# A cross-attention and mixture-of-experts kernel: the second layer's shared products in two halves, and batch 2 routed by itself

## The chip, the core and the metric

The kernel runs on one core of one Trainium2 chip. The metric is the time of one execution on the device, in microseconds. The core has five engines that run side by side: TensorE (PE, matrix products, with its weight loads shown as PEld), VectorE (DVE), ScalarE (ACT), GpSimd (POOL) and SyncE (SP, which here issues most DMAs). Each engine works through its own instructions in the order in which they are written; between engines there are only semaphores.

## The reference

1024 tokens (4 batches of 256) of width 256 pass through four stages, each added to the running sum: attention over a 1601-token context, a mixture of experts (16 experts, 6 per token), a 16-head attention over the same context, and a second mixture of experts with 16 experts of width 128, two per token, and a shared expert of width 256 that every token passes. The change lies in the last stage and at the end of the third:

```python
def _L1_ffn_ref(x, router_w, router_bias, Wu, Wg, Wd, Su, Sg, Sd):
    flat = x.reshape(Bx * Tx, D)
    logits = flat @ router_w.T
    scores = jax.nn.softmax(logits, axis=-1)
    _, topk_idx = jax.lax.top_k(logits + router_bias, TOPK)      # TOPK = 2
    topk_scores = jnp.take_along_axis(scores, topk_idx, axis=-1)
    topk_scores = topk_scores / topk_scores.sum(-1, keepdims=True)
    ...
    for e in range(N_EXPERTS):                                    # 16
        h = jax.nn.silu(flat @ Wu[e]) * (flat @ Wg[e])
        out = out + combine[:, e:e + 1] * (h @ Wd[e])
    for s in range(N_SHARED):                                     # 1
        out = out + jax.nn.silu(flat @ Su[s]) * (flat @ Sg[s]) @ Sd[s]
x = x + _L1_xattn_ref(_layernorm(x), ...)
x = x + _L1_ffn_ref(_layernorm(x), ...)
```

## The kernel before

**Attention of the third stage.** Its work is cut into 16 jobs (4 batches of 4 groups of 4 heads), a job into 13 tiles of 128 context tokens: 208 tiles x. For each tile TensorE forms scores (`qk`, L881), ScalarE takes the exponential (L1279), VectorE clips it (`clip`, L1659) and TensorE multiplies it with the values four tiles later (`pv`, L915). Three PSUM buffers of scores and six buffers of exponentials link them. After a job VectorE copies the product out (`evac`, tile oS, L1665), TensorE transposes it (`flip`, L923) and VectorE divides (`norm`, tile cx).

**What happens to a finished batch.** While the next batch runs, the functions `between` of each engine fit the finished batch's rest between the tiles, by a written table of tile numbers o (0 to 51 within a batch): transposes of cx (`ctx_T`), the output product (`ctx_out`, L937), bias (`delta`, L1681), its statistics, scale and sum (`delta_gamma` L1695, `delta_add` L1701), the mean of the sum (`rows_mean`, L1710), the normalized rows xe (`rows`, L1718) and their transposes (`rows_T`, L944) into xTh (ScalarE, `rows_hi`, L1259) and xTl (VectorE, `rows_lo`, L1723), the two parts of a split 32-bit number. The inverse roots are computed by GpSimd in small steps (`inverse_root`, L351 to L359); VectorE waits for them in `delta_add` and `rows`. One batch later come the router products (`logits`, L646 to L648), the choice of two experts per token (15 operations, L1744 to L1768), TensorE's counts of earlier tokens (`ranks`, L960, L963), the slot numbers (`slots_of`, `slots_to`, L1772 to L1780), and GpSimd's scatters of the rows into DRAM slots sorted by expert (`rows_out`, L621): two 128-token tiles of a batch, two experts each, are four scatters.

**The end.** Batch 3 has nothing to hide behind. Its steps follow each other in the open, and the choice of batch 2 is made together with it, over four tiles, with eight scatters. The shared expert comes in the same place. Its two weight tiles are loaded into e_w when all attention is done; GpSimd splits them into sh_hi and sh_lo (L633, L635). TensorE starts all output banks with 16 products of zeros (L1015), then runs four chunks n (weight tile n // 2, tokens 512 (n % 2) and the 511 behind them): six gate products, six up products (`shared_hidden`), and 12 down products of the chunk before (`shared_down`). ScalarE and VectorE make silu, h, hh and hl of each chunk. In between VectorE computes the table of blocks: 31 blocks of up to 128 slots of one expert, of which SyncE reads its row numbers and TensorE its expert numbers. VectorE then computes the mixing weights (softmax, L1920 to L1930) and adds the shared output to resid (L1934). Only when that is done (`add_rdy` 8) does TensorE take the first block: transposes of its rows (`slots_T`, L1064), gate and up (L1078), transpose (L1086), down (L1092). VectorE copies the block out (yb, L1949), GpSimd scatters it to the tokens (L641). After the last one SyncE loads the rows back (yg) and VectorE mixes them, two operations a tile (L1963, L1965), into resid, which is stored.

Of the kernel before, what the change touches and what calls it, by code (L numbers as in the profile page):

```python
# [15 lines left out]
F32 = mybir.dt.float32  # L16
F32R = mybir.dt.float32r
# [59 lines left out]
def build(nc, a, out, stop="D"):  # L77
# [8 lines left out]
    with ExitStack() as ctx:  # L86
# [76 lines left out]
        with ExitStack() as s:  # L163
# [8 lines left out]
            wq_raw = C("wq_raw", [P, KT, D])  # L172
            wqh, wql = C("wqh", [P, KT, D], F32R), C("wql", [P, KT, D], F32R)
            wo_raw = C("wo_raw", [P, KT, D])
# [8 lines left out]
        with ExitStack() as s:  # L183
# [6 lines left out]
            silu_d = Dt("silu_d", [P, 2, 512])  # L190
            h32_d = Dt("h32_d", [P, 2, 512])
            hh_d, hl_d = Dt("hh_d", [P, 2, 512], F32R), Dt("hl_d", [P, 2, 512], F32R)
# [6 lines left out]
            Dt("gap2", [P, 400])  # L199
            sh_hi, sh_lo = Dt("sh_hi", [P, NSH1, WC], F32R), Dt("sh_lo", [P, NSH1, WC], F32R)  # L200
            Dt("gap3", [P, 13500])
# [9 lines left out]
            m_c, m_t, m_p, m_e, m_l = (Dt(n, [P, NT, E]) for n in ("m_c", "m_t", "m_p", "m_e", "m_l"))  # L211
# [8 lines left out]
            eb_f = Dt("eb_f", [P, NBLK])  # L220
            eb_i = Dt("eb_i", [P, NBLK], I32)
            eb_r = Dt("eb_r", [P, NBLK])
            tok = Dt("tok", [P, NT])
            y_c = Dt("y_c", [P, NBLK])
            y_i = Dt("y_i", [P, NBLK], I32)
            first_row = Dt("first_row", [P, E])
            aside = Dt("aside", [P, NBLK])
            ob, rb_f = Dt("ob", [P, NBLK]), Dt("rb_f", [P, NBLK])
            rb_i = Dt("rb_i", [P, NBLK], I32)

        cTxh, cTxl = (t[:].rearrange("p k n -> p (k n)").rearrange("p (q n) -> p q n", n=512) for t in (xTh, xTl))
        dlt = xn
        cTf = wq_raw[:].rearrange("p k n -> p (k n)")
# [128 lines left out]
        def _(sp):  # L362
# [154 lines left out]
            for g in range(NG - 1):  # L517
                queries(0, g)
            for job in range(KSL, NJ):
# [11 lines left out]
            for k in range(NSH1):  # L531
                sp.dma_start(e_w[:, k, :], a["w1"][k]).then_inc(d_in[0], 16)
# [30 lines left out]
        def _(pool):  # L563
# [87 lines left out]
        def _(pe):  # L651
# [315 lines left out]
            def between(y):  # L967
# [10 lines left out]
                if 0 <= b < NB - 1:  # L978
# [24 lines left out]

            t = NT - 2
# [1023 lines left out]
```

## Time and profile before

| | us |
|---|---|
| median of 3 runs | 817.32 (817.09 to 819.99) |
| the profiled execution | 816.02 |
| its span, first to last instruction | 814.2 |
| PE busy | 707.8 (87%) |
| DVE busy | 543.3 (67%) |
| ACT busy | 396.5 (49%) |
| POOL busy | 160.1 (20%) |
| attention of the third stage, first to last exponential | 463.8 to 686.5 |
| first expert block taken up by PE | 741.05 |
| last block copied out | 795.37 |

Busy time is an average over stages with different limits. A matmul's record includes its way through the array, so records of successive products overlap; the chain of waits gives each only the time up to the next. The granted clock of TensorE is given as a share of full speed: 1.0 is 2.4 GHz, 0.50 is 1.2 GHz. Its mean over the span is 0.95.

### The profile page before, as it was taken

How to read it: one execution, taken by the hardware profiler on the slowest of the kernel's cores; microseconds unless marked ns; L12 is line 12 of the kernel's file. 1: busy time of each engine (PE TensorE's matmuls, PEld its weight loads, DVE VectorE, ACT ScalarE, POOL GpSimd, SP SyncE). 2: the span in 40 equal slices, each digit the busy share in tenths (PEclk: the TensorE clock that was granted, in tenths of full speed). 3: DMA queues.
4: the chain of work that ended last, by engine and by line, in shares of the span. 5: the costliest groups of instructions: out<-in, count | busy, mean ns of one | idle time of the engine just before them, and what ended most of it. 6: DMA issues, size and time to landing. Idle time of an engine off the chain costs nothing.

```text
span 814.2 us, 14794 instructions
## 1 busy us (share of the span) xinstructions
PE 707.8 (87%) x5481; PEld 537.1 (66%) x5481; DVE 543.3 (67%) x1124; ACT 396.5 (49%) x558; POOL 160.1 (20%) x196
## 2 busy tenths in 40 slices
PE   4799999897859999999995599998998997587990
PEld 3689888796648888888885344454554554475880
DVE  6765565656676666666676377778888886655663
ACT  2624333233312322223322499999999996114540
POOL 5452625030100000000000000004024024231561
PEclk9999999998989999999998789999999998698995
DMA  7465464735306776767779369898687700812545
GB/s 231 129 208 214 162 220 130 270 104 178 96 23 221 238 248 206 262 211 245 240 172 198 60 112 191 133 127 166 96 137 144 108 2 30 345 53 74 162 144 180
DMA packets 57532, 131.67 MB, mean 162 GB/s; under 512 B 12433, under 2 KB 32785, under 8 KB 53889
## 3 DMA queue, kind: packets, MB, share of 16 engines
q1 hardware_dynamic: 54208, 123.46, 57.1%
q0 software_dynamic: 2256, 6.18, 2.1%
q10 hardware_dynamic: 1008, 1.25, 0.5%
q8 instruction: 37, 0.61, 0.4%
q14 instruction: 23, 0.18, 0.1%
HBM read 78.92 MB, written 48.79 MB: 157 GB/s over the span
## 4 chain that ended last, share of the span: by engine, by line
PE 53%; DVE 15%; issue 10%; ACT 9%; POOL 7%; DMA 4%; SPq 1%; POOLq 0%; DVEq 0%; ACTq 0%
PE ps L646 13%; PE ps L647 13%; PE ps L648 13%; ACT p L1279 5%; PE ps L915 5%; PE ps L881 3%; POOL y_tokens L641 3%; DVE p L1659 2%; DMA raw<-in_ctxT 1%; PE ps L1078 1%; DMA raw<-in_ctxN 1%; ACT cNh L1156 1%; PE ps L937 1%; PE ps L723 1%; POOL na L354 1%
## 5 line engine op out<-in xcount | busy, mean ns | idle before, releaser
L1279 ACT ACTIVATE p<-ps,kbias 128x1024 f32<-128x1024 f32 (+1 forms) x208 | 210.5, 1184 | 6.2 <-PE ps L881 6.2
L1659 DVE TENSOR_SCALAR p<-p 128x1024 f32<-128x1024 f32 (+1 forms) x208 | 142.6, 692 | 40.0 <-ACT p L1279 38.4
L915 PE MATMUL ps<-p,vsl 128*17 128x256 f32 (+1 forms) x1664 | 116.7, 392 | 3.6 <-DVE p L1659 3.6
L881 PEld LDWEIGHTS ps<-qst,kst 48*128 48x128 f32 (+1 forms) x832 | 60.4, 187 | 67.3 <-issue 34.6
L881 PE MATMUL ps<-qst,kst 48*128 48x256 f32 (+1 forms) x832 | 93.4, 324 | 11.5 <-DMA qst<-ql 5.9
L1219 ACT ACTIVATE hh<-h 128x512 fp32r<-128x512 f32 x50 | 31.6, 632 | 137.7 <-DVE h L1591 113.9
L351 POOL TENSOR_SCALAR nv<-mv 128x2 f32<-128x2 f32 x6 | 3.4, 561 | 423.7 <-DVE mv L1691 407.7
L646 PE MATMUL ps<-xTh,w_hi 128*128 128x512 f32 x200 | 80.0, 400 | 5.2 <-DVE h L1587 4.5
L648 PE MATMUL ps<-xTh,w_lo 128*128 128x512 f32 x200 | 79.3, 397 | 0.0
L647 PE MATMUL ps<-xTl,w_hi 128*128 128x512 f32 x200 | 79.2, 396 | 0.0
L915 PEld LDWEIGHTS ps<-p,vsl 128*17 128x17 f32 (+1 forms) x1664 | 37.2, 98 | 43.0 <-issue 9.1
L1593 DVE TENSOR_TENSOR hl<-h,hh 128x512 fp32r<-128x512 f32 x50 | 34.6, 692 | 36.6 <-ACT hh L1219 36.6
L646 PE MATMUL ps<-w_hi,hh 128*128 128x256 f32 x200 | 57.5, 288 | 1.5 <-DVE hl L1593 1.5
L1587 DVE TENSOR_TENSOR h<-silu,ps 128x512 f32<-128x512 f32 x50 | 34.4, 688 | 35.4 <-PE ps L648 23.2
L647 PE MATMUL ps<-w_lo,hh 128*128 128x256 f32 x200 | 57.2, 286 | 0.0
L648 PE MATMUL ps<-w_hi,hl 128*128 128x256 f32 x200 | 57.0, 285 | 0.0
L646 PEld LDWEIGHTS ps<-xTh,w_hi 128*128 128x128 f32 x200 | 37.9, 190 | 13.5 <-DVE h L1587 5.8
L589 POOL TENSOR_TENSOR cNl<-raw,cNh 128x1024 fp32r<-128x1024 f32 (+1 forms) x16 | 31.3, 1980 | 77.8 <-ACT cNh L1156 77.8
L648 PEld LDWEIGHTS ps<-xTh,w_lo 128*128 128x128 f32 x200 | 37.8, 189 | 9.0
L647 PEld LDWEIGHTS ps<-xTl,w_hi 128*128 128x128 f32 x200 | 37.9, 189 | 6.6
L646 PEld LDWEIGHTS ps<-w_hi,hh 128*128 128x128 f32 x200 | 38.7, 193 | 4.2 <-DVE hl L1593 1.9
L1215 ACT ACTIVATE silu<-ps 128x512 f32<-128x512 f32 x50 | 29.9, 598 | 21.6 <-PE ps L648 20.9
(290 smaller groups left out, 1530.0 us busy)
## 6 DMA issues: line engine op xcount, KB each, us to landing
x_slots<-blank SPq DMA_DIRECT2D x20, 1032.0 KB, 6.0
kst<-k_hi SPq DMA_DIRECT2D x64, 200.2 KB, 7.8
w_raw<-in_w SPq DMA_DIRECT2D x25, 384.0 KB, 3.6
v_one<-vst SPq DMA_DIRECT2D x4, 1768.0 KB, 9.0
vsl<-v_one SPq DMA_DIRECT2D x4, 1768.0 KB, 16.5
kst<-k_lo SPq DMA_DIRECT2D x32, 200.2 KB, 8.2
raw<-in_ctxN SPq DMA_DIRECT2D x12, 512.0 KB, 5.6
k_hi<-kh SPq DMA_DIRECT2D x24, 256.0 KB, 2.6
```

Source lines behind the costliest of these rows:

```text
L589: pool.tensor_tensor(cNl[:, c0:c0 + w, :], src, cNh[:, c0:c0 + w, :].bitcast(F32), ALU.subtract).then_inc(ctx_split, 1)
L646: e.matmul(o, lh, rh, start=first, stop=False, skip_group_check=True)
L647: e.matmul(o, lh, rl, start=False, stop=False, skip_group_check=True)
L648: return e.matmul(o, ll, rh, start=False, stop=last, skip_group_check=True)
L881: mm = pe.matmul(ps[0:rows, 2 * (x % RING) + t, c * SEQ:(c + 1) * SEQ], kst[r, job % KSL, c, m * P:m * P + rows], qst[r, b, 2 * g + c, :], ...
L915: mm = pe.matmul(ps[32 * j:32 * j + VW, 6 + job % 2, 0:SEQ], vsl[0:rows, b % 2, at_:at_ + VW], p32[0:rows, x % PBUF, (2 * t + c) * SEQ:(2 ...
L1215: act.activation(silu[:, half, :], ps[:, 4, :], ACT.Silu).then_inc(silu_rdy, 1)
L1219: act.activation(hh[:, half, :], h32[:, half, :], ACT.Copy).then_inc(hh_rdy, 1)
L1279: act.activation(p32[0:rows, x % PBUF, :], psf[0:rows, bank * 512:bank * 512 + 1024], ACT.Exp, scale=0.25, bias=kbias[0:rows, col:col + 1] ...
L1587: dve.tensor_tensor(h32[:, half, :], silu[:, half, :], ps[:, 5, :], ALU.mult).then_inc(mul1_rdy, 1)
L1593: dve.tensor_tensor(hl[:, half, :], h32[:, half, :], hh[:, half, :].bitcast(F32), ALU.subtract).then_inc(hl_rdy, 1)
L1659: dve.tensor_scalar(t, t, CLO, CHI, ALU.max, ALU.min).then_inc(p_clip, 1)
```

## The change

1. The shared weights are loaded at the start of the third stage's attention (SyncE, behind three groups of queries and ahead of keys(3)) into the tile xn, which is free then. VectorE splits them in job 2, tiles m = 2 to 9, one part per tile; GpSimd splits none.
2. In `between`, the mean of a batch's sum moves from o = 39 to 38, `rows` from 43 and 45 to 45 and 46, `rows_T` on TensorE from 49 to 51, `rows_hi` from 49 to 50, `rows_lo` from 50 to 51.
3. Batch 2 is chosen and ranked by itself (`choose`, two tiles), ahead of batch 3's `delta`; its four scatters are issued before batch 3's.
4. Tokens 0 to 511 get their gate and up products around the last transposes, and their down products after the counts. The 16 products of zeros go: each output is a full accumulation of its own now. Their sums (`shared_add` 0 and 1) stand ahead of the blocks.
5. Tokens 512 to 1023 get theirs behind the last block. The exponential and the mixing weights move there too; the sums of these tokens stand between the mix of tile 3 and that of tile 4.

```diff
+            sp.wait_ge(sc_rdy, 1)
+            for k in range(NSH1):
+                sp.dma_start(sh_raw[:, k * WC:(k + 1) * WC], a["w1"][k]).then_inc(d_in[0], 16)
             for job in range(KSL, NJ):
...
             sp.wait_ge(cx_rdy, NJ)
-            for k in range(NSH1):
-                sp.dma_start(e_w[:, k, :], a["w1"][k]).then_inc(d_in[0], 16)
...
-            for k in range(NSH1):
-                pool.wait_ge(d_in[0], 16 * NSH1)
-                pool.tensor_copy(sh_hi[:, k, :], e_w[:, k, :]).then_inc(d_w, 1)
-                pool.wait_ge(d_w, 2 * k + 1)
-                pool.tensor_tensor(sh_lo[:, k, :], e_w[:, k, :], sh_hi[:, k, :].bitcast(F32), ALU.subtract).then_inc(d_w, 1)
+            rows_out(NB - 1, NT - 4, NT - 2)
             pool.wait_ge(ln_xn, 4 * NT)
-            rows_out(NB - 1, NT - 4, NT)
+            rows_out(NB, NT - 2, NT)
...
-                    elif o == 49:
+                    elif o == 51:
                         pe.wait_ge(cx_rdy, y // MT)
                         rows_T(t, 2, spare)
...
+            logits(NB - 2, ps[:, 5, :])
             pe.wait_ge(cx_rdy, NJ)
             for j in range(2):
                 ctx_T(t + j, 1, ps[:, j, :])
-            logits(NB - 2, ps[:, 7, :])
             for j in range(2):
                 ctx_out(t + j, j, 1, ps[:, 2 + j, 0:D])
+            ranks(NB - 1, NT - 4, NT - 2, ps[:, 1, :])
+            pe.wait_ge(d_w, 8)
+            gates(0, 0, 4)
+            ups(0, 0, 5)
+            gates(0, 1, 6)
+            pe.wait_ge(dl_ev, NT)
             for j in range(2):
-                rows_T(t + j, 1, ps[:, 4 + j, :])
-            logits(NB - 1, ps[:, 7, 2 * E:])
-            for n in range(4 * 4):
-                pe.matmul(psf[:, n * P:(n + 1) * P], zero[:], zero[:], start=True, stop=False, skip_group_check=True)
+                rows_T(t + j, 1, ps[:, 2 + j, :])
+            ups(0, 1, 0)
+            logits(NB - 1, ps[:, 7, :])
+            pe.wait_ge(pre_ev, NB - 1)
+            ranks(NB, NT - 2, NT, ps[:, 1, :])
+            pe.wait_ge(lg_ev, NB)
+            all_counts(ps[:, 7, 2 * E:3 * E])
+            pe.wait_ge(hl_rdy, SC0 + 2)
+            shared_down(0, 2)
-            shared_hidden(0)
-            ranks(NB - 1, NT - 4, NT, ps[:, 6, :])
-            all_counts()
-            for n in range(1, 2 * NSH1):
-                shared_hidden(n)
-                shared_down(n - 1)
-            shared_down(2 * NSH1 - 1)
...
-            pe.wait_ge(add_rdy, 8)
             for j in range(-2, NBLK + 1):
...
+            gates(1, 0, 0)
+            ups(1, 0, 1)
+            gates(1, 1, 2)
+            ups(1, 1, 3)
+            pe.wait_ge(hl_rdy, SC0 + 4)
+            shared_down(1, 4)
...
-                    elif o == 39:
+                    elif o == 38:
                         rows_mean(b)
-                    elif o == 43:
+                    elif o == 45:
                         rows(t)
-                    elif o == 45:
+                    elif o == 46:
                         rows(t + 1)
-                    elif o == 50:
+                    elif o == 51:
                         rows_lo(t, 2, spare)
...
+                if job == 2 and 2 <= m < 10:
+                    (shared_hi if m < 6 else shared_lo)(m)
...
+            choose(t - 2, t, ps[:, 5, :])
             for j in range(2):
                 delta(t + j, 1, ps[:, 2 + j, :])
...
+            shared_mul(0, 5)
+            choose(t, NT, ps[:, 7, :])
+            shared_mul(1, 0)
...
             for t in range(NT):
+                if t == NT // 2:
+                    shared_add(2, 4)
+                    shared_add(3, 5)
```

Here `gates(h, k, bank)` and `ups(h, k, bank)` are six products each with weight tile k for token half h, and `shared_down(h, bank)` 24 products over both weight tiles.

TensorE, from the last output product to the counts, in the kernel before (wo_raw: output weights; xe: normalized rows; gwh_d: router weights; zero: zeros; sh_hi: shared weights; sel: the choice):

```order
L937 MATMUL ps<-wo_raw,wq_raw 128x256 x4
L944 MATMUL ps<-ident,xe 128x128 x4
L646 MATMUL ps<-gwh_d,xTh 128x16
...
L1015 MATMUL ps<-zero 128x128 x16
L646 MATMUL ps<-xTh,sh_hi 128x512
...
L960 MATMUL ps<-sel,upper 128x64
```

And in the changed kernel:

```order
L939 MATMUL ps<-wo_raw,wq_raw 128x256 x4
L962 MATMUL ps<-sel,upper 128x32
...
L648 MATMUL ps<-xTh,sh_hi 128x512
L649 MATMUL ps<-xTl,sh_hi 128x512
L650 MATMUL ps<-xTh,sh_gl 128x512
...
L946 MATMUL ps<-ident,xe 128x128 x4
...
L648 MATMUL ps<-gwh_d,xTh 128x16
...
L962 MATMUL ps<-sel,upper 128x32
```

Batch 2's ranks and 18 shared products moved ahead of the last transposes; six more stand behind them, and nothing but the router products stands between those and batch 3's ranks.

VectorE, from the last division to the statistics of batch 3, in the kernel before (cx: attention output; xn: delta):

```order
L1677 TENSOR_TENSOR cx<-ps,r4 128x2x64
L1681 SCALAR_TENSOR_TENSOR xn<-ps,rs,bo 128x256
L1686 BN_STATS st6<-xn 128x6
L1681 SCALAR_TENSOR_TENSOR xn<-ps,rs,bo 128x256
```

And in the changed kernel (m_l to sel: the choice of batch 2):

```order
L1695 TENSOR_TENSOR cx<-ps,r4 128x2x64
L1778 COPY m_l<-ps 128x32
L1782 TENSOR_TENSOR m_c<-m_l,gb_d 128x32
L1786 TENSOR_REDUCE m_top<-m_c 128x2
L1787 TENSOR_TENSOR m_t<-m_c,m_top 128x32
...
L1802 TENSOR_TENSOR sel<-one1,one2 128x32
L1699 SCALAR_TENSOR_TENSOR xn<-ps,rs,bo 128x256
```

Fifteen operations of the choice have come between cx and delta.

VectorE behind the last block copies, in the changed kernel; before, the mix followed the copies (yb) at once:

```order
L1985 COPY yb<-ps 128x256 x3
L1929 TENSOR_TENSOR h32_d<-silu_d,ps 128x512 x2
L1933 TENSOR_TENSOR hl_d<-h32_d,hh_d 128x512 x2
L2000 TENSOR_REDUCE m_sum<-m_p 128x8
...
L2010 TENSOR_TENSOR m_w2<-m_w2,m_top 128x8
L2019 SCALAR_TENSOR_TENSOR resid<-yg,m_w1,resid 128x256
```

The second half's h and hl and eleven operations of the mixing weights now stand between the copies and the mix.

## Rows read from the trace of the kernel before

**Rows 1.** Timeline, ScalarE: start us, us, engine, line, operation, idle before it and releaser.
```profile
569.40 0.60 ACT L1259 ACTIVATE xTh<-ps 128x512 fp32r<-128x512 f32 x1 [0.53 <-PE ps L944]
...
625.72 0.60 ACT L1259 ACTIVATE xTh<-ps 128x512 fp32r<-128x512 f32 x1 [1.16 <-PE ps L944]
...
682.75 0.60 ACT L1259 ACTIVATE xTh<-ps 128x512 fp32r<-128x512 f32 x1 [1.79 <-PE ps L944]
684.41 2.11 ACT L1279 ACTIVATE p<-ps,kbias 128x1024 f32<-128x1024 f32 x2 [1.06 <-PE ps L881]
```

**Rows 2.** Timeline, VectorE: batch 2's first rows, and the last copy oS.
```profile
678.68 0.41 DVE L1718 TENSOR_SCALAR xe<-resid,mv,rstd 128x256 f32<-128x256 f32 x1 [2.02 <-POOL rstd L359]
...
689.05 0.42 DVE L1665 COPY oS<-ps 128x256 f32<-128x256 f32 x1 [1.60 <-PE ps L915]
```

**Rows 3.** Page, costliest groups: line, operation, xcount, busy us, mean ns, idle before.
```profile
L1593 DVE TENSOR_TENSOR hl<-h,hh 128x512 fp32r<-128x512 f32 x50 | 34.6, 692 | 36.6 <-ACT hh L1219 36.6
```

**Rows 4.** Chain that ended last, 686 to 741 us: start us, us in chain, what.
```profile
693.75 0.49 DVE xn L1681
...
702.43 1.28 ACT L1292
...
712.85 0.43 PE ps L646
...
718.24 0.17 DVE pos_i L1780
...
730.29 0.23 PE ps L646
```

**Rows 5.** Lines L1695 and L1701 (min/median/max ns), then the timeline beside them.
```profile
L1695 DVE SCALAR_TENSOR_TENSOR xn<-xn,mv,gam x8: 477/480/2024, 550.6 to 696.2; 128x256 f32<-128x256 f32 x8
...
L1701 DVE SCALAR_TENSOR_TENSOR resid<-xn,rstd,resid x8: 478/485/2016, 555.6 to 699.1; 128x256 f32<-128x256 f32 x8
...
699.00 1.86 POOL L635 TENSOR_TENSOR sh_lo<-e_w,sh_hi 128x768 fp32r<-128x768 f32 x1
...
702.65 0.74 DVE L1718 TENSOR_SCALAR xe<-resid,mv,rstd 128x256 f32<-128x256 f32 x2
```

**Rows 6.** Timeline, VectorE: first and last of the 15 operations of the choice.
```profile
708.00 0.22 DVE L1744 COPY m_l<-ps 128x64 f32<-128x64 f32 x1 [2.89 <-PE ps L648]
...
711.54 0.23 DVE L1768 TENSOR_TENSOR sel<-one 128x64 fp32r<-128x64 f32 x1
```

**Rows 7.** Timeline: first and last of eight scatters, first block loads, first block.
```profile
719.28 1.01 POOL L621 DMA_INDIRECT x_slots<-xe,pos_i  x1 [18.42 <-DVE pos_i L1780]
...
728.22 1.01 POOL L621 DMA_INDIRECT x_slots<-xe,pos_i  x1 [0.30 <-issue]
...
731.76 3.73 SPq L544 DMA_DIRECT2D xb<-x_slots  x4
...
741.05 1.12 PE L1064 MATMUL ps<-ident,xb 128*128 128x128 f32 x4 [4.75 <-DVE resid L1934]
```

**Rows 8.** Chain around the mixing weights, then VectorE's timeline of the tail.
```profile
735.50 0.30 DVE m_sum L1920
...
738.51 2.49 DVE resid L1934 x4
...
794.95 0.42 DVE L1949 COPY yb<-ps 128x256 f32<-128x256 f32 x1 [0.16 <-PE ps L1092]
...
803.27 0.48 DVE L1963 SCALAR_TENSOR_TENSOR resid<-yg,m_w,resid 128x256 f32<-128x256 f32 x1 [7.89 <-DMA yg<-y_tokens]
...
811.12 0.48 DVE L1965 SCALAR_TENSOR_TENSOR resid<-yg,m_w,resid 128x256 f32<-128x256 f32 x1
```

**Rows 9.** A stretch (PE, PEld, DVE, ACT, POOL busy; PEclk, DMA share, GB/s); DMA issues to landing.
```profile
698.00:700.00 2.00, 0.00 (x0) 0.00 (x0) 1.96 (x4) 0.00 (x0) 1.92 (x2) 0.50 1.03 415
...
e_w<-in_w SPq DMA_DIRECT2D x2, 3072.0 KB, 17.1
...
raw<-in_ctxN SPq DMA_DIRECT2D x4, 128.0 KB, 3.6
```

More of the change, by code:

```diff
@@ L1002, in _, with gates, ups, shared_down @@
             flip(NJ - 1)
+            def gates(h, k, bank):
+                s = slice(h * 512, h * 512 + 512)
+                for q in range(KT):
+                    w = slice(q * 2 * P, q * 2 * P + P)
+                    mm = mm3(pe, ps[:, bank, :], sh_hi[:, k, w], sh_gl[:, k, w], xTh[:, q, s], xTl[:, q, s], q == 0, q == 1)
+                mm.then_inc(G_rdy, 1)
+            def ups(h, k, bank):
+                s = slice(h * 512, h * 512 + 512)
+                for q in range(KT):
+                    w = slice(q * 2 * P + P, (q + 1) * 2 * P)
+                    mm = mm3(pe, ps[:, bank, :], sh_hi[:, k, w], sh_gl[:, k, w], xTh[:, q, s], xTl[:, q, s], q == 0, q == 1)
+                mm.then_inc(U_rdy, 1)
+            def shared_down(h, bank):
+                for j in range(4):
+                    o = ps[:, bank + j // 2, (j % 2) * D:(j % 2 + 1) * D]
+                    s = slice(j * P, (j + 1) * P)
+                    for k in range(NSH1):
+                        mm = mm3(pe, o, hh_d[:, 2 * h + k, s], hl_d[:, 2 * h + k, s],
+                                 sh_hi[:, k, 2 * D:3 * D], sh_dl[:, k, :], k == 0, k == NSH1 - 1)
+                mm.then_inc(down_done, 1)
+            def all_counts(o):
+                for t in range(NT):
+                    mm = pe.matmul(o, ones[:], sel[:, t, :], start=t == 0, stop=t == NT - 1, skip_group_check=True)
+                mm.then_inc(pre_rdy, 1)
             t = NT - 2
+            logits(NB - 2, ps[:, 5, :])
             pe.wait_ge(cx_rdy, NJ)
@@ L1033, in shared_down @@
-            def shared_down(n):
-                k, half = n // 2, n % 2
-                pe.wait_ge(hl_rdy, SC0 + n + 1)
-                for j in range(4):
-                    t, s = 4 * half + j, slice(j * P, (j + 1) * P)
-                    mm = mm3(pe, ps[:, t // 2, (t % 2) * D:(t % 2 + 1) * D], hh_d[:, half, s], hl_d[:, half, s],
-                             sh_hi[:, k, 2 * D:3 * D], sh_lo[:, k, 2 * D:3 * D], False, False)
-                mm.then_inc(down_done, 1)
-            def all_counts():
-                cnt = ps[:, 7, 4 * E:5 * E]
-                for t in range(NT):
-                    mm = pe.matmul(cnt, ones[:], sel[:, t, :], start=t == 0, stop=t == NT - 1, skip_group_check=True)
-                mm.then_inc(pre_rdy, 1)
@@ L1268, in between @@
                         ctx_ev(t, 2, spare)
-                    elif o == 49:
+                    elif o == 50:
                         rows_hi(t, 2, spare)
@@ L1854, in _, with choose @@
             b, t = NB - 1, NT - 2
+            def choose(t0, t1, o):
+                logits_ev(t0, t1, o)
+                biased(t0, t1)
+                max_equal(t0, t1)
+                max_first(t0, t1, one1)
+                take_first(t0, t1)
+                max_equal(t0, t1)
+                max_first(t0, t1, one2)
+                take_both(t0, t1)
+            choose(t - 2, t, ps[:, 5, :])
             for j in range(2):
```

175 lines of the change are left out of this document (93 added, 82 removed).

## The prediction, on record before the changed kernel ran

> **What bounds the kernel now.** I read the timeline of each engine around the last attention tiles first, then the chain of waits from there to the end, then the timeline of the scatters and of the last 20 us. In attention ScalarE's exponentials run nearly without a gap; the reader should look for the places where they do not. ScalarE waits for the transposes of a finished batch's normalized rows: 0.53, 1.16 and 1.79 us in front of the copies xTh, and another 1.06 us behind the last one [rows 1]. Their cause is one wait further back: VectorE stood 2.02 us for the root that GpSimd computes [rows 2]. I call A the start of VectorE's last copy oS, 689.05 [rows 2], and A' the same point of the changed kernel. From A everything is one chain of small steps: delta of the last batch starts at A+4.70 [rows 4], its normalized rows end at 703.39 = A+14.34 [rows 5], the slot numbers at 718.41 = A+29.36 [rows 4]; GpSimd issues eight scatters; SyncE fetches the first block at 731.76 = A+42.71, and TensorE takes it up only at 741.05 = A+52.00 [rows 7], because the shared sum of VectorE ends at 738.51+2.49 = 741.00 [rows 8]. The expert blocks run to 795.37, the mix to 811.60 [rows 8], and the span ends at 814.2. So TensorE's shared products are no longer hidden work: they stand in front of the slot numbers and in front of the first block.
>
> The sums below are against the profiled execution: 816.02 us, its span 814.2 and 1.8 around it. The median of the runs is 817.32, 1.3 more, and I add that at the end.
>
> **1. Attention.** For batches 0 to 2 the mean moves one tile earlier and the rows two tiles later, so the root gets three tiles (3 us) more; it was 2.02 us late. TensorE transposes two tiles later, ScalarE copies one tile later. I expect no wait for the root. In batch 2 the 1.79 + 1.06 = 2.85 us go, and some 0.5 us of the products that queued up behind the stall before the last 1.60 us wait [rows 2]: 3.3 us. In batches 0 and 1, 0.53 + 1.16 = 1.7 us stand in the rows; I count 1.2. Against it: the shared weights are split on VectorE now, four casts and four subtractions of 512 and 256 columns in eight tiles of job 2. A subtraction of 512 takes 692 ns [rows 3]; the 256-wide ones at half and casts no dearer make 0.69 x 6 = 4.2 us at most, while clip and exponential leave about 0.3 us per tile, 2.4 us in eight tiles. A backlog of 2 us is more than one tile, and I charge 0.7 us (bounds 0, where the ring of six buffers takes it up, and 3). Their loads stand on SyncE's queue before keys(3), which are wanted a dozen tiles later: nothing. Gain 3.8 us.
>
> **2. From A to the last rows.** GpSimd splits no weights here any more. Two kinds of fused operation, xn and resid, take 480 and 485 ns in the median, but their slowest took 2024 and 2016 ns, with GpSimd's sh_lo subtraction of 1.86 us beside them [rows 5]. Over the four of batch 3 that is 5.2 us instead of 1.95, so 3.26 us go. The Trainium skill (SBUF — State Buffer, "Who interferes with whom") says that a VectorE instruction with two SBUF inputs and a GpSimd one that reads SBUF shut each other out for the whole instruction; by that rule the trace agrees, and all of it goes. The other reading would be the expert weights' DMA, which fills all 16 queues in these microseconds (share 1.03, [rows 9]); under it the two xe operations still took 0.74 us together [rows 5], so I don't take it.
> The choice of batch 2 now stands between cx and delta on VectorE. Fifteen operations of the choice over four tiles took 708.00 to 711.77, 3.77 us [rows 6]; over two tiles each is some 35 ns shorter, 3.25 us. TensorE's router product for it comes first after the flip and ends near A+2.3, so the choice ends at A+5.65, and delta, ready at A+4.1, starts 0.95 later than A+4.70. ctx_T waits 0.5 us behind the router products and stays hidden. The rows end at 14.34 - 3.26 + 0.95 = A+12.0; 0.2 us for joints: gain 2.1 us.
>
> **3. From the rows to the slot numbers.** Before, 15.0 us, with TensorE's 16 zero products in them, and then the first gate and up products at the low clock (0.43 us each in the chain against 0.23 at the high one, [rows 4]) in front of the ranks. Now the gate and up products of tokens 0 to 511 run from about A+6.5: 18 x 0.23 = 4.2 us before the last transposes, ending near A+10.7, when TensorE waits for the rows anyway, and six more (1.4 us) beside ScalarE's table load and the two xTl. What stays in the chain: transposes, table load and copies to the last xTl 1.75 (as before), router products 1.35, choice 3.25, TensorE's ranks or VectorE's product h 0.95, three slot operations and their links 0.87, three more 0.65, joints 0.2: 9.0 us. Gain 6.0 us. It needs TensorE at the high clock through A+10.
>
> **4. Scatters.** Eight scatters start 1.277 us apart (719.28 to 728.22 is seven steps, [rows 7]). Four of them, batch 2's, now start near A+15.6 and are issued by A+20.7, before batch 3's slot numbers at A+21. Four fewer in the chain: 5.1 us. VectorE's block table (5.5 us, after two hl of 1.4 us) ends 1.3 us before the last scatter lands, so it is hidden, just. SyncE is let go at 42.71 - 2.1 - 6.0 - 5.1 = A'+29.5. Expert weights are issued behind cx and land 17.1 us later [rows 9], before that.
>
> **5. From SyncE's release to the first block.** Before, 9.29 us [rows 7], nearly all of it shared products. Now only the slot rows' own load counts. The trace doesn't show its landing; a load of 128 KB took 3.6 us [rows 9], and it cannot be below 0. I take 3.0: gain 6.3 us (bounds 5.7 and 9.3). The first-half sums (2 x 0.62 us) end near A'+30. All blocks together I leave at 795.37 - 741.05 = 54.3 us.
>
> **6. The tail.** Here the change pays. L is the end of the last block's copy, 795.37; the first pair of the mix started at 803.27 = L+7.9 and the last ended at L+16.2 [rows 8], waiting for transfers, with TensorE idle. Now 24 products of 0.23 us start near L-0.4 and end at L+5.3; h, hh and hl of the last chunk (about 0.7 each) end at L+7.5; 24 down products of half the columns, 2.8 us, end at L+10.3. Beside these ScalarE loads the exponential's table (1.28, as the table load of [rows 4]) and VectorE computes the mixing weights: L+8.4 + 3.0 (735.50 to 738.51, [rows 8]) = L+11.4. Then four tiles of mix 3.7, two sums 1.25, four tiles 3.7: L+20.1. Cost 3.9 us; down products and transfers are covered.
>
> **Sum.** 3.8 + 2.1 + 6.0 + 5.1 + 6.3 - 3.9 = 19.4 us; 816.02 - 19.4 = 796.6, and against the median 817.32 it is 797.9 us.
>
> **Rivals.**
> (a) Low clock. With TensorE idle between the delta products and the transposes the granted clock fell to 0.50 [rows 9], 1.2 GHz, and the chain's gate products then cost 0.43 us [rows 4]. Against it: TensorE's idle time before its shared products falls to about 1.7 us, for the choice of batch 2. If it does happen, 18 products end at A+14.2, 2.2 us after the rows, and six gate products, router products and ranks cost 2.5 more: 4.7, so 802.6. Chance 0.13.
> (b) Attention gives nothing: the backlog of the split stalls ScalarE for 3 us and the moved transposes only shift their wait. 3.8 is lost: 801.7; with a small loss beside, 803. Chance 0.10.
> (c) The early scatters don't get out of the way: their rows queue behind the expert weights in full DMA engines until about A+18, GpSimd is held, and eight scatters stand in the chain as before. +5.1: 803.0. Chance 0.07. The Trainium skill has a rule on this side (SBUF — State Buffer, the "DVE blocks DMA" warning): VectorE copies can lock GpSimd out of writing descriptors. Here the eight scatters kept their even steps beside a busy VectorE; by that rule a few tenths of a microsecond might come on each, within (c).
> (d) The slow fused operations were the DMA's: 3.3 us stay: 801.2. Chance 0.04.
> (e) Slower than before: TensorE enters the blocks after about 6 us of idling (A'+25.5 to A'+32) where it was 4.75 [rows 7], and stays at the low clock in the loop. A block is 54.3/31 = 1.75 us and TensorE-bound at the high clock; at the low one about 1.6 us are added. From 12 of 31 blocks on the 19.4 are gone; with 16, 823. Against it: the loop before started from idling as well and took hardly more than its steady pace. Chance 0.03.
>
> **How the numbers follow.** Forecast 0.63 (795 to 800.5), (a) to (e) as above. Likeliest time 797.9. The range goes down by the transfer's other bound and attention's full 1.7, to 793.5, and up to take in (a) to (c): 803.5. A measurement of this kernel tells about 0.5% (4 us) from no change; faster by more holds in all cases but (e) and unforeseen ones: 0.95; within 0.5%: 0.02; slower 0.03.
>
> **What would show it.** No ScalarE gap over 0.5 us at the xTh copies; A' at 684 to 686; no fused operation above 0.6 us behind it; TensorE's clock 1.0 during the gate products; batch 2's four scatters issued before batch 3's slot numbers; the first block 31 to 34 us behind A'; the last mix 19 to 21 us behind the last block copy. A first block later than A'+37, or TensorE at 0.5 in the loop, would make the forecast wrong.

## The result, and the profile after

The changed kernel takes 796.06 us (median of 4 runs, 794.48 to 798.38) where the one before took 817.21 beside it: a ratio of 0.974, with a 95% interval of 0.970 to 0.978. Six further runs on another chip gave 798.49 (795.26 to 799.97) and 0.9747 (0.9716 to 0.9778). The forecast was 797.9, the range 793.5 to 803.5. The profiled execution took 794.68 us; its span is 792.8, 21.4 shorter than before.

I cut both spans at the same points: the start of attention (ScalarE's first exponential), A (the last copy oS), the end of the last normalized rows xe, the last slot numbers pos_i, the first block on TensorE, L (the end of the last block's copy) and the last mix.

| stretch | before | after | gain | forecast |
|---|---|---|---|---|
| up to the start of attention | 463.76 | 465.42 | -1.66 | 0 |
| attention, to A | 225.29 | 218.32 | 6.97 | 3.8 |
| A to the last rows | 14.34 | 11.65 | 2.69 | 2.1 |
| rows to slot numbers | 15.02 | 10.03 | 4.99 | 6.0 |
| slot numbers to first block | 22.64 | 10.99 | 11.65 | 5.1 + 6.3 |
| blocks, to L | 54.32 | 53.89 | 0.43 | 0 |
| L to the last mix | 16.23 | 19.96 | -3.73 | -3.9 |

The sum is 21.3; the rest is behind the last mix. Nothing was changed ahead of the start of attention: it lies between 463.6 and 467.6 us in the fourteen profiled executions of this document, so the -1.66 is spread between executions. The page's busy times (busy us, share of the span, instructions by engine) read:
```profile
PE 708.5 (89%) x5471; PEld 537.7 (68%) x5471; DVE 544.1 (69%) x1153; ACT 394.7 (50%) x557; POOL 163.3 (21%) x192
```
TensorE is busy for 708.5 us where it was for 707.8, now 89% of the shorter span. But for the 16 products of zeros the work is the same, so what went was waiting. ScalarE's timeline of the changed kernel at the three copies xTh, which answers to [rows 1]:
```profile
571.33 0.70 ACT L1268 ACTIVATE xTh<-ps 128x512 fp32r<-128x512 f32 x1
...
625.94 0.70 ACT L1268 ACTIVATE xTh<-ps 128x512 fp32r<-128x512 f32 x1
...
680.60 0.67 ACT L1268 ACTIVATE xTh<-ps 128x512 fp32r<-128x512 f32 x1
681.09 1.18 ACT L1288 ACTIVATE p<-ps,kbias 65x1024 f32<-65x1024 f32 x1
```
No bracket stands behind any of them: the view shows no wait in front of the copies. ScalarE's waits from the start of attention to A show the whole of it, first of before, then of after (engine, line, what it waited for: us in total, times, longest):
```profile
ACT p L1279 <- PE ps L881: 6.2, 13, 1.1
ACT xTh L1259 <- PE ps L944: 3.5, 3, 1.8
```
```profile
ACT p L1288 <- PE ps L883: 4.3, 10, 0.6
```
9.7 us of waiting have become 4.3. The last oS also follows the last exponential 1.06 us sooner.

VectorE's timeline, beside [rows 2, 5 and 6]:
```profile
678.22 0.41 DVE L1736 TENSOR_SCALAR xe<-resid,mv,rstd 128x256 f32<-128x256 f32 x1 [0.92 <-POOL rstd L364]
...
683.74 0.42 DVE L1683 COPY oS<-ps 128x256 f32<-128x256 f32 x1
...
685.94 0.19 DVE L1778 COPY m_l<-ps 128x32 f32<-128x32 f32 x1 [0.51 <-PE ps L650]
...
689.05 0.19 DVE L1802 TENSOR_TENSOR sel<-one 128x32 fp32r<-128x32 f32 x1
689.16 0.48 DVE L1699 SCALAR_TENSOR_TENSOR xn<-ps,rs,bo 128x256 f32<-128x256 f32 x1
...
691.27 0.88 DVE L1713 SCALAR_TENSOR_TENSOR xn<-xn,mv,gam 128x256 f32<-128x256 f32 x2
...
692.26 0.88 DVE L1719 SCALAR_TENSOR_TENSOR resid<-xn,rstd,resid 128x256 f32<-128x256 f32 x2
```
The root is still late, by 0.92 us instead of 2.02 (the prediction expected no wait for it), but the copies behind it no longer wait. Batch 2's choice ends at A'+5.5 and delta starts behind it. The fused operations xn and resid take 0.88 us for two, 1.76 for the four; before they took 5.2.

TensorE's granted clock, in stretches of 2 us (columns as in [rows 9]):
```profile
687.74:689.74 2.00, 2.00 (x8) 1.59 (x7) 1.76 (x10) 0.00 (x0) 0.00 (x0) 0.61 0.92 310
689.74:691.74 2.00, 2.00 (x14) 1.75 (x13) 1.93 (x7) 0.30 (x1) 0.00 (x0) 1.00 1.02 415
...
699.74:701.74 2.00, 0.00 (x0) 0.00 (x0) 1.72 (x10) 0.00 (x0) 1.70 (x2) 0.50 1.03 402
```
Its gate and up products did run at 1.00 (2.4 GHz), beside a DMA share of 1.02. But TensorE then idled 3.44 us for batch 3's choice, and the clock was 0.50 at the ranks. The timeline from the last transposes to the first block, beside [rows 7]:
```profile
695.21 0.68 PE L946 MATMUL ps<-ident,xe 128*128 128x128 f32 x4 [0.34 <-DVE xe L1736]
...
698.35 0.97 POOL L627 DMA_INDIRECT x_slots<-xe,pos_i  x1 [11.96 <-DVE pos_i L1814]
...
702.33 1.64 PE L965 MATMUL ps<-sel,ones 128*128 128x32 f32 x7
...
704.01 0.19 DVE L1806 TENSOR_TENSOR m_t<-ps,first_row 128x32 f32<-128x32 f32 x1 [1.39 <-PE ps L965]
...
706.29 1.17 POOL L627 DMA_INDIRECT x_slots<-xe,pos_i  x1 [3.14 <-DVE pos_i L1814]
...
710.32 1.32 POOL L627 DMA_INDIRECT x_slots<-xe,pos_i  x1 [0.30 <-issue]
...
712.59 1.28 DVE L1967 TENSOR_TENSOR resid<-resid,ps 128x512 f32<-128x512 f32 x2
...
714.17 4.91 SPq L550 DMA_DIRECT2D xb<-x_slots  x5
...
716.41 0.69 PE L1066 MATMUL ps<-ident,xb 128*128 128x128 f32 x2 [5.26 <-DMA xb<-x_slots]
```
The 18 products end at A'+11.1, and TensorE waits 0.34 us for the rows behind them: here they stand in nobody's way. Four scatters are out before batch 3's slot numbers; what the first block waits for is no longer VectorE's sum (done at 713.87) but its own load, 2.24 us behind SyncE's release. No run puts the shared products of tokens 512 to 1023 back in front of the blocks, so what their move is worth is read from these two traces alone (9.29 us from the release to the first block before, 2.24 now). The tail, on ScalarE and VectorE, beside [rows 8]:
```profile
769.88 0.42 DVE L1985 COPY yb<-ps 128x256 f32<-128x256 f32 x1 [0.16 <-PE ps L1096]
...
776.86 1.28 ACT L1342 ACT_TABLE_LOAD   x1
...
778.50 0.29 DVE L2000 TENSOR_REDUCE m_sum<-m_p 128x8 f32<-128x128 f32 x1 [0.93 <-ACT m_p L1342]
...
781.52 0.48 DVE L2019 SCALAR_TENSOR_TENSOR resid<-yg,m_w,resid 128x256 f32<-128x256 f32 x1
...
785.19 1.28 DVE L1967 TENSOR_TENSOR resid<-resid,ps 128x512 f32<-128x512 f32 x2
...
789.78 0.48 DVE L2021 SCALAR_TENSOR_TENSOR resid<-yg,m_w,resid 128x256 f32<-128x256 f32 x1
```
The mix no longer waits for the gathered rows: the table load and the weights stand in front of it.

### The profile page after: what moved, and what is told of

Same layout as the page of the kernel before. It is cut to its first block, busy times and chain, and to the rows that moved or that the text cites. A ratio compares the mean times of both kernels' runs of the same rounds, so it can differ in the third digit from the quotient of the medians.

```text
span 792.8 us, 14800 instructions
## 1 busy us (share of the span) xinstructions
PE 708.5 (89%) x5471; PEld 537.7 (68%) x5471; DVE 544.1 (69%) x1153; ACT 394.7 (50%) x557; POOL 163.3 (21%) x192
## 4 chain that ended last, share of the span: by engine, by line
PE 53%; ACT 12%; DVE 10%; issue 10%; DMA 8%; POOL 4%; SPq 3%; ACTq 0%; DVEq 0%; POOLq 0%
PE ps L648 12%; PE ps L649 12%; PE ps L650 12%; ACT p L1288 8%; PE ps L917 4%; PE ps L1082 3%; PE ps L883 3%; DMA raw<-in_ctxT 2%; DMA qst<-ql 2%; PE ps L1096 2%; POOL cTl L608 2%; SPq L508 2%; DMA raw<-in_ctxN 2%; DMA k_lo<-kl 1%; ACT cNh L1165 1%
## 5 line engine op out<-in xcount | busy, mean ns | idle before, releaser
L356 POOL TENSOR_SCALAR nv<-mv 128x2 f32<-128x2 f32 x6 | 5.1, 850 | 416.6 <-DVE mv L1709 402.4
```

## Experiments

In each, stretches of the profiled execution are read as in the table above; the times are medians with the ratio to the kernel before on the same chip.

**1. The order between the attention tiles.** e1 puts only the new table into the kernel before; e2 only the mean and the rows of VectorE, not its copies xTl; e3 takes the table out of the changed kernel.
```diff
 # e1 and e2, in the kernel before: VectorE's mean and rows
-                    elif o == 39:
+                    elif o == 38:
                         rows_mean(b)
-                    elif o == 43:
+                    elif o == 45:
                         rows(t)
-                    elif o == 45:
+                    elif o == 46:
                         rows(t + 1)
 # e1 only: TensorE's transposes, then ScalarE's copies, then VectorE's
-                    elif o == 49:
+                    elif o == 51:
...
-                    elif o == 49:
+                    elif o == 50:
                         rows_hi(t, 2, spare)
...
-                    elif o == 50:
+                    elif o == 51:
                         rows_lo(t, 2, spare)
```


> The kernel before with only the new order of the work between the attention tiles: mean one tile earlier, normalized rows, transposes and their copies later, on VectorE, TensorE and ScalarE. Nothing is moved of the shared weights, products, scatters. Theory (the table makes the whole gain of attention, since a late root and its copies held ScalarE in every batch): attention start to the last copy oS falls from 225.3 us to about 218.3, the time by 7 us, near 810. Rival (my forecast's size, 4.5 us without the weight split, and the rest came with GpSimd's relief or noise): 220.8 us, 812.7. Rival (the table gives nothing alone): 225, 817.

> The kernel before with only VectorE's part of that order (mean one tile earlier, rows two tiles later); TensorE's transposes and ScalarE's copies stay where they were. The transposes then come while the rows are still being made, so they and the copies xTh must wait. Theory (the places on all three engines count together): no gain in attention or a loss, 225 to 229 us from its start to the last oS. Rival (only the wait for the root counted): 218 to 220 us, as with the whole order.

> The changed kernel with only the order between the attention tiles put back. Theory (attention's gain is the table's, and the rest of the change stands by itself): 7 us slower than the changed kernel, 803; attention start to last oS 225 us; from there on nothing changes. If the weight split on VectorE costs something that the new order hides: more than 225.3 us. Rival (the gain came from elsewhere, GpSimd without weight casts): 0 to 2.5 us slower.

| kernel | attention to A, us | median, us | ratio (95%) |
|---|---|---|---|
| before | 225.29 | 818.99 | |
| e1, the table alone | 218.15 | 811.59 | 0.9924 (0.9891 to 0.9957) |
| e2, VectorE's part alone | 224.62 | 816.63 | 0.9965 (0.9938 to 0.9991) |
| changed kernel | 218.32 | 796.06 | 0.974 (0.970 to 0.978) |
| e3, changed, old table | 225.63 | 806.09 | 0.9844 (0.9799 to 0.989) |

(The changed kernel was measured on another chip; the median of the kernel before is that of the chip of e1 to e3.) e1 has all 7 us and e3 has none. The weight split on VectorE, the only other thing in this stretch that changed, would be the difference between e1 and the changed kernel (0.17 us), or between e3 and before (0.34). Both are smaller than what executions of this stretch differ by (218.14 to 219.45 us in the ten with table and split), so no cost of it is shown. e2 gains 0.7 us in the trace, which is within that spread too, and 2.4 us in the median, where e1 gains 7.4; the expectation was no gain. Its waits of ScalarE are:
```profile
ACT p L1279 <- PE ps L881: 5.4, 13, 0.7
ACT xTh L1259 <- PE ps L944: 2.3, 3, 0.9
```
An earlier mean helps the root, but the transposes come while the rows are unfinished, and TensorE, working in order, holds the scores behind them. VectorE's part alone is thus not enough. A run with the later transposes and copies alone was not made, so whether VectorE's part is needed beside them isn't shown.

**2. The early scatters.** e4 issues batch 2's four together with batch 3's.
```diff
-            rows_out(NB - 1, NT - 4, NT - 2)
             pool.wait_ge(ln_xn, 4 * NT)
-            rows_out(NB, NT - 2, NT)
+            rows_out(NB, NT - 4, NT)
```


> The changed kernel with batch 2's four scatters issued together with batch 3's, behind the last slot numbers. Theory (the scatters' steps on GpSimd stand in the chain): four steps of 1.277 us more between the slot numbers and the first block, +5.1 us, 801.2. Rival (the first block is held by something else, such as the block table or the expert weights): 0 to 2 us.

The timeline of e4, GpSimd's last scatter and SyncE's first load:
```profile
717.20 0.97 POOL L627 DMA_INDIRECT x_slots<-xe,pos_i  x1 [0.30 <-issue]
...
720.88 4.91 SPq L550 DMA_DIRECT2D xb<-x_slots  x5
```
From the slot numbers to the first block it takes 16.26 us instead of 10.99: 5.27, the forecast's four steps. The median is 801.62, ratio 0.9774 (0.9726 to 0.9823); the times alone would leave 2.8 us with an uncertainty larger than that, so it is the trace that decides.

**3. Why the fused operations had been slow.** e5 adds two GpSimd subtractions that read SBUF beside xn and resid of the last batch; e6 adds six fills there. Both write a scratch tile and change no result. The cuts leave out the tile's definition and the semaphores by which each one waits for the one before.
```diff
 # e5
+            pool.wait_ge(dl_st, NT)
+            for k in range(2):
+                pool.tensor_tensor(idle_out, sh_hi[:, 0, :].bitcast(F32), sh_hi[:, 1, :].bitcast(F32), ALU.subtract)...
 # e6
+            pool.wait_ge(dl_st, NT)
+            for k in range(6):
+                pool.memset(idle_out, 0.0)...
```


> The changed kernel with two GpSimd subtractions of 128x768 added that read SBUF, beside the fused operations xn and resid of the last batch; they write a scratch tile that nothing reads. Theory (while GpSimd works on two SBUF operands, VectorE's fused operation with two SBUF inputs waits): those fused operations that meet one take up to 2 us instead of 0.48, the rows end some 3 us later, and with them the first block. Rival (the slow ones were the fault of the expert weights' transfers, which are there in the changed kernel too): all of them stay at about 0.48 us.

> The control to the run with GpSimd's subtractions: in the same place six GpSimd fills of 128x768, that write SBUF and read nothing from it. Theory (two reading engines shut each other out): xn and resid stay at about 0.48 us, the first block is not later. Rival (any work of GpSimd on SBUF slows them): above 1 us, as in the other run.

Timelines of e5, VectorE and GpSimd:
```profile
693.85 3.89 DVE L1718 SCALAR_TENSOR_TENSOR xn<-xn,mv,gam 128x256 f32<-128x256 f32 x2
...
697.85 0.88 DVE L1724 SCALAR_TENSOR_TENSOR resid<-xn,rstd,resid 128x256 f32<-128x256 f32 x2
...
693.69 3.77 POOL L640 TENSOR_TENSOR yb<-sh_hi 128x768 f32<-128x768 f32 x2 [5.69 <-DVE st L1709]
```
and of e6:
```profile
693.96 0.88 DVE L1718 SCALAR_TENSOR_TENSOR xn<-xn,mv,gam 128x256 f32<-128x256 f32 x2
...
697.34 1.32 DVE L1741 TENSOR_SCALAR xe<-resid,mv,rstd 128x256 f32<-128x256 f32 x2
...
693.76 4.75 POOL L640 MEMSET yb<- 128x768 f32 x6 [6.28 <-DVE st L1709]
```
In e5 two xn take 3.89 us, in e6 0.88, with the same expert weights in flight. resid of e5, behind GpSimd's end, takes 0.88 again. So it is GpSimd's reads that stop VectorE's operation, 3.0 us for two, and not the transfers: rival (d) is refuted, and the rule that the prediction cites (the Trainium skill, SBUF — State Buffer, "Who interferes with whom") is borne out here for GpSimd subtractions against scalar_tensor_tensor. The rows end 2.5 us later in e5 (15.63 behind A) than in e6 (13.12). Each of the two ran once, in 801.41 and 799.44 us, so their times say nothing beside this trace.

**4. Are the first half's products free where they stand?** e10 puts the 24 gate and up products behind the last counts. VectorE's part goes with them: its products h and rests hl now follow the table of blocks, where h had stood around batch 3's choice and hl behind the slot numbers.
```diff
 # TensorE
-            gates(0, 0, 4)
-            ups(0, 0, 5)
-            gates(0, 1, 6)
...
-            ups(0, 1, 0)
...
             all_counts(ps[:, 7, 2 * E:3 * E])
+            pe.wait_ge(d_w, 8)
+            gates(0, 0, 4)
+            ups(0, 0, 5)
+            gates(0, 1, 6)
+            ups(0, 1, 0)
 # VectorE
-            shared_mul(0, 5)
             choose(t, NT, ps[:, 7, :])
-            shared_mul(1, 0)
...
-            shared_low(0)
-            shared_low(1)
...
+            shared_mul(0, 5)
+            shared_mul(1, 0)
+            shared_low(0)
+            shared_low(1)
```


> The changed kernel with the gate and up products of tokens 0 to 511 (24 on TensorE, their two products h and rests hl on VectorE) put behind the last counts, where batch 3's ranks no longer wait for them. Everything else stays. Theory (in the changed kernel these products are free, since TensorE waits there for the last rows): the slot numbers come no earlier or 0.5 us earlier, the shared sums of the first half end some 5 to 8 us later, behind SyncE's release, and the first block starts 2 to 6 us later: 799 to 802. Rival (the products hold up the slot numbers as much as they are worth): no change, within 1 us.

TensorE's clock in e10 while it waits for the rows, and its timeline at the first down product and the first block:
```profile
692.00:694.00 2.00, 0.00 (x0) 0.00 (x0) 1.60 (x7) 0.41 (x2) 0.00 (x0) 0.50 1.03 413
```
```profile
716.72 0.38 PE L648 MATMUL ps<-sh_hi,hh_d 128*128 128x256 f32 x1 [2.24 <-DVE hl_d L1933]
...
720.79 1.03 PE L1066 MATMUL ps<-ident,xb 128*128 128x128 f32 x4
```
The slot numbers come 11.43 us behind the rows instead of 10.03: TensorE stands idle in the products' place and does the rest of the chain at 0.50. The first block starts at A+38.47, 5.8 us later, behind the down products, which waited for VectorE's hl. Median 803.72, ratio 0.983 (0.979 to 0.9871); the profiled execution, 798.93, was the fastest of its four. So the products cost 5.8 us in the other place. That they are free where the change put them is read from the changed kernel's own trace, where TensorE waits for the rows behind them. e10 can't say it: its clock had fallen at A+1.8, before the first thing that it changes. The execution that compares with it is that of e8 (experiment 5), with the products in place and the clock at 0.50 from A+1.8 too: slot numbers at A+24.35, against A+23.96 in e10. At the low clock, then, the products are not quite free.

**5. Can the tail's cost be had back, and the clock?** e7 puts the exponential and the mixing weights back in front of the blocks; e11 does so too, with ScalarE waiting for the scatters first; e8 fills two idle gaps of TensorE with zero products; e12 is e11 with e8's first gap filled. The zero products wait for the first silu of tokens 0 to 511. after_again is the changed kernel, unedited.
```diff
 # e7, e11 and e12 (shortened): ScalarE in front of the blocks, and
 # VectorE's eleven operations behind shared_add
+            act.wait_ge(pos_rdy, NB + 1)
+            act.wait_ge(slots_out, 16 * 2 * NT)              # e11 and e12 only
+            act.activation(m_p, m_e, ACT.Exp)
+            act.activation(std[:, 0:1], eps[:], ACT.Silu)    # its table again
...
 # e8 and e12, TensorE behind logits(3); e8 also 40 behind shared_down(0)
+            pe.wait_ge(silu_rdy, SC0 + 1)
+            for n in range(26):
+                pe.matmul(ps[:, 4, 0:P], zero[:], zero[:], start=True, stop=True, skip_group_check=True)
```


> The changed kernel with the exponential and VectorE's eleven operations of the mixing weights put back in front of the expert blocks, where VectorE and ScalarE now wait for the first load; one small Silu behind the exponential brings its table back. The shared sums of the second half stay behind the blocks. Theory (in the tail the table load and the weights stand between the sums and the mix): the last mix ends 17 to 17.5 us behind the last block copy instead of 19.96, the time falls by 2.5 to 3 us, 793.3. Rival (the down products or the gathered rows end last there): 0 to 1 us. Rival (the two table loads delay the first block's Silu): the blocks start or run 1.3 us later and half of it is lost.

> The changed kernel with zero products of 128 columns added in two gaps of TensorE: 26 behind the last router products, 40 behind the down products ahead of the first block. They add nothing to any result. Theory (the granted clock of 0.50 at the ranks and in the first blocks follows from TensorE idling before them): clock 1.0 there, ranks 0.8 us shorter, first blocks 1 to 1.5 us shorter, in all 2 us, 794. Rival (the ranks wait for VectorE anyway and the first blocks for their loads): 0 to 0.5 us.

> As the run with the mixing weights ahead of the blocks, but ScalarE's exponential waits until the last slot rows have landed. In the first such run the tail was 2.6 us shorter, but SyncE was let go 5.85 us behind the last scatter's start instead of 3.85. Theory (the table load and VectorE's small operations beside the last scatter held its transfer): SyncE is let go 3.7 to 4.3 us behind the last scatter's start again, the first block is at most 0.5 us later than in the changed kernel, the tail stays at 17.4 us, and the time is 2 to 2.5 us below the changed kernel's on the same chip. Rival (the 2 us belonged to that execution or to the program's layout): the release is late again, or it is not and nothing can be told from VectorE's place.

> The former kernel with the 26 zero products of 128 columns ahead of the ranks of batch 3 alone (the 40 ahead of the blocks, which did not hold the clock, are left out). Theory (they keep the granted clock up at the ranks when it was up before them): ranks 0.93 instead of 1.64 us, 0.7 us less. Rival (where the clock was at 0.50 at the gate products, the zero products only stand in the way): no difference in the median, or slower by up to 1 us.

> The changed kernel once more, beside the others on the same chip: is what differs between two executions of the same kernel as large as the differences of 1 to 2 us that the zero products and the weights were to make? Expected: median 795 to 799; attention 218.3 +-0.4 us, the slot numbers 21.7 us behind the last oS where TensorE's clock is 1.0 at the delta products and up to 2 us later where it is 0.50; tail 19.96.

| kernel | A to slots | last scatter to SyncE | A to block 1 | blocks | tail | median, us | ratio (95%) |
|---|---|---|---|---|---|---|---|
| changed | 21.68 | 3.85 | 32.67 | 53.89 | 19.96 | 796.06 | 0.974 (0.970 to 0.978) |
| after_again | 21.68 | 5.14 | 33.74 | 58.86 | 19.99 | 798.49 | 0.9747 (0.9716 to 0.9778) |
| e7 | 21.61 | 5.85 | 34.50 | 55.04 | 17.37 | 795.78 | 0.9738 (0.9701 to 0.9775) |
| e8 | 24.35 | 4.34 | 35.79 | 54.62 | 19.98 | 799.19 | 0.9762 (0.9727 to 0.9798) |
| e11 | 23.01 | 3.88 | 33.94 | 57.44 | 17.38 | 796.70 | 0.9721 (0.9682 to 0.976) |
| e12 | 21.87 | 3.89 | 32.94 | 56.03 | 17.28 | 797.84 | 0.9749 (0.9714 to 0.9783) |

(Stretches in us; "A to slots" goes to the last slot numbers, "last scatter to SyncE" from the last scatter's start to SyncE's first load of slot rows.) The tail is 2.6 us shorter in all three kernels with early weights, and no more, since the mix then waits for the gathered rows again. e7's tail is as it was forecast; its time, 795.78, is 2.5 us above the forecast 793.3. e7's chain of waits:
```profile
777.58 2.42 DMA y_tokens<-yb,y_i
...
780.58 3.85 DMA yg<-y_tokens
...
784.53 0.49 DVE resid L2020
```
The median doesn't show the 2.6 us clearly: e11 is 1.8 us below after_again on the same chip, their intervals overlap, and no version is shown faster than the changed kernel. after_again says why: two executions of one kernel differ by 1.3 us in the release of SyncE and by 5.0 us in the blocks. A late release comes without the weights beside the last scatter too, so neither e7's 5.85 nor e11's return to 3.88 shows that they had a part in it.

The 5.0 us in the blocks have two parts. The first copy comes out 8.1 us behind the first block instead of 6.9 (the clock went back to 1.00 only 5.9 us into the blocks, against 3.6). Up to the 13th block the copies then follow each other every 1.63 us in both. The other 3.8 us lie behind it, where the 14th comes after 2.6 us instead of 1.67 and further waits follow. Six of the eleven executions with these blocks have that 2.6 at the 14th (after_again, e7, e8, e10, e11, e12). There engines stand for reasons that the trace doesn't name, as here (ScalarE, then VectorE behind it):
```profile
759.07 0.28 ACT L1324 ACTIVATE sb_<-ps 128x128 f32<-128x128 f32 x1 [1.13 <-remote]
...
759.38 0.29 DVE L1974 TENSOR_TENSOR hb<-sb_,ps 128x128 f32<-128x128 f32 x1 [2.40 <-ACT sb_ L1324]
```
Their cause stays open.

The zero products did in e8 what they were to do at the ranks, 0.93 us for seven instead of 1.64. But TensorE's clock of e8 had been at 0.50 since A+2, though from A+2 to A+4 it was busy for 1.95 us, and for all of every stretch of 2 us behind it up to A+14:
```profile
693.73:695.73 2.00, 2.00 (x7) 1.61 (x7) 1.93 (x8) 0.30 (x1) 0.00 (x0) 0.50 1.03 418
695.73:697.73 2.00, 2.00 (x6) 1.61 (x5) 1.57 (x7) 0.73 (x2) 0.00 (x0) 0.50 1.03 407
697.73:699.73 2.00, 2.00 (x10) 1.59 (x9) 1.00 (x5) 1.05 (x2) 0.00 (x0) 0.99 1.04 406
```
```profile
699.88 0.60 PE L946 MATMUL ps<-ident,xe 128*128 128x128 f32 x4
```
```profile
719.73:721.73 2.00, 0.89 (x9) 0.75 (x7) 0.21 (x1) 0.00 (x0) 0.00 (x0) 0.98 0.34 83
721.73:723.73 2.00, 1.45 (x6) 0.96 (x6) 0.65 (x3) 0.71 (x2) 0.00 (x0) 0.50 0.46 119
```
The gate products then ended at A+14.3, not A+11, and held up the transposes, which follow them without a wait, and the router products: 11.8 us from the rows to the slot numbers instead of 10.0. That is rival (a) in the very place where the prediction put it, in an execution of a kernel that is the changed one up to there. The 40 products ahead of the blocks did not keep the clock: TensorE idled only 1.11 us behind them, and it was 0.50 from 0.1 us into the first block on. So e8's theory is half wrong, and its time, forecast at 794, was 799.19. In e12 the seven ranks took 1.29 us, half of the gain, and its median is not below that of e11.

Across the executions the slot numbers go with the time at which the clock came back. It fell to 0.50 between A+1.3 and A+2.2 in nine of the eleven. It was back at 1.00 from A+5.3 to A+5.6 on in three (the changed kernel twice, e12), and in two it hadn't fallen there (e3, e7): slot numbers at A+21.6 to A+21.9. It came back at A+8.1 in e4 and e11: delta's products ended at A+7.6 instead of A+6.3, the rows at A+13.0 and the slot numbers at A+23.0. It came back at A+12.0 in e6 and e8, with slot numbers at A+24.2 and A+24.4. Up to there each engine has the same instructions in e4, e8 and e11 as in the changed kernel; why the clock came back at different times isn't shown.

## Why the prediction was right

- **The chain from A, cut into stretches.** Right in its mechanism but for TensorE's clock at the ranks (term 3). Scatters: four steps forecast, 5.1 us, and 5.27 us in e4. Products hidden in front of the last rows: TensorE waited 0.34 us for the rows behind them, and in the other place they cost 5.8 us (e10). Fused operations held by GpSimd: shown by e5 and e6. Batch 2's choice in front of delta: it ended at A'+5.5 (forecast 5.65).
- **Term 1, attention, was mis-sized:** 3.8 forecast, 6.97 measured, and A' came at 683.7, just ahead of the 684 to 686 that the prediction gave as a sign. The mechanism, late roots that hold TensorE's transposes and with them ScalarE, is what e1 and e3 bear out, though the root kept 0.92 us of its wait. The errors point the same way. I charged 0.7 us for the weight split, of which nothing is shown (experiment 1). I counted 1.2 of the 1.7 us of batches 0 and 1. Of ScalarE's waits for scores 1.9 us went, where I had counted only the one of 1.06: they queued behind the waiting transposes on TensorE. And 1.06 went between the last exponential and A, where I had put 0.5. What went adds up to 3.5 + 1.9 + 1.06 = 6.5; half a microsecond I can't place.
- **Term 3 was 1.0 too large:** it took the high clock all the way. The gate products had it, the ranks did not, after 3.44 us of idling. The sum itself contained that idling (the choice, 3.25 us), and I did not draw the conclusion. VectorE waited 1.39 us for the ranks.
- **Term 5:** the load took 2.24 us instead of the 3.0 chosen.
- **The sum** came near because these errors differ in sign: attention gave 3.2 us more than forecast, the stretches from A to the first block 0.2 less, while the start of attention was 1.7 later for reasons outside the change. That part is luck.
- **Blocks:** "left at 54.3" was right for this execution by luck. Eleven profiled executions with the same blocks gave 53.8 to 58.9, a spread as large as the largest terms that I worked out.
- **Tail:** -3.9 forecast, -3.7 measured, and by the steps named: weights, not products or transfers, end last. e7 confirms it by taking them away.
- **The lower end of the range** is 0.9 us lower than its two named terms give: 797.9 less 3.0 for the load and 0.5 for attention is 794.4. The result, 796.06, doesn't hang on it.
- **Rivals.** (b) is refuted by e1 and e3, (d) by e5 and e6. (c) is refuted by the trace, in which batch 2's four scatters started 1.27 to 1.28 us apart from 698.35 on and were out by 703.15, before batch 3's slot numbers at 705.42, and by e4. (e) did not come: the clock was back at 1.00 3.6 us into the blocks. (a) did not come in the profiled executions of the changed kernel, but in those of e8 and e6, where the clock was 0.50 until A+12.0 and the gate products ended behind the rows (11.84 and 11.06 us from the rows to the slot numbers, instead of 10.03). In e4 and e11 the low clock, until A+8.1, cost 1.4 us in front of the rows and nothing behind them, which the prediction had not considered. Its chance of 0.13 was too low for such mild forms: the slot numbers came 21.6 to 21.9 us behind A in five executions (the changed kernel twice, e3, e7, e12) and 23.0 to 24.4 in five (e4, e6, e8, e10, e11; e10 changes this stretch itself, and e6 adds fills). e5, whose subtractions hold up the rows, is not counted. At its full price of 4.7 us (a) came in none.

## What to carry to other kernels

Read a late step back to the engine that works in order: its wait is paid by everything queued behind it. Roots that came up to 2 us late in three batches cost 7 us, and moving one engine's part of the remedy gave a tenth of that in the trace and a third in the medians. Put independent products where an engine waits anyway: in the changed kernel they cost nothing there, though at the low clock they can outlast the wait (e8). TensorE's clock did not stay up over a gap of 3 us behind them. Before chasing 2 us in a kernel of 800, profile the same kernel twice and compare by stretches.

## What the runs showed of the hardware that I had not expected

- The granted clock was 0.50 for 10 us while TensorE was busy for all but 0.05 us (e8, A+2 to A+12), where the same instructions in the changed kernel had 1.00 from A+6. Idling before is thus not the only condition; two executions of the same code need not agree.
- GpSimd's fills, which read nothing, left scalar_tensor_tensor alone (0.88 us for two) but not tensor_scalar: two xe took 1.32 us beside them (e6) and 0.74 without. The Trainium skill (SBUF — State Buffer, "Who interferes with whom") has a second rule, for VectorE's two-port modes against any work of GpSimd, that would fit; no run here shows in which mode xe is.
- Two GpSimd subtractions of 128x768 took 3.77 us in e5, 1.9 each, as the 1.86 of [rows 5]: while VectorE stood for them, GpSimd ran at its usual pace.
